# Choosing experts inside the attention stage ahead of the mixture of experts

## The reference, cut to what matters

```python
def diffusion(x):                        # third layer, per batch of 512 tokens
    x = x + token_diffusion(ln(x)) * gamma1     # 16 heads, softmax over 512 x 512 squared distances
    x = x + channel_diffusion(ln(x)) * gamma2   # 8 heads over 32 x 32 channels
    return x

def experts(x):                          # fourth layer, all 4096 tokens
    gates = softmax(x @ gate_w)                 # 8 experts
    topw, topi = top_k(gates, 2); topw = topw / sum(topw)
    h = gelu(ln(x @ w1[e] + b1[e]))             # 256 -> 512, for the two chosen experts
    y = h @ w2[e] + b2[e]                       # 512 -> 256
    return ln(sum_k(topw_k * y_k) + x)
x = x + ln(diffusion(ln(x)))
x = x + ln(experts(ln(x)))
```

## Time and profile before

| | |
|---|---|
| time, median of 3 runs | 4168.49 us (4158.25 to 4170.33) |
| the profiled execution | 4168.6 us, its span 4166.9 us |
| mean granted TensorE clock | 0.945 |
| attention stage, one body of the loop | 96.00 us |
| attention stage, last body, then drain | 90.80 us, 75.20 us |
| choosing and plan, until the first block's rows are there | 116.00 us |
| the 71 blocks | 301.20 us |
| the end | 108.90 us |

### The profile page before, as it was taken

The page is one execution under the profiler, slowest core; times in us unless marked ns, Lnnn a source line. Parts: engine busy times, 40 slices in busy tenths (PEclk is TensorE's granted clock), DMA queues, the critical chain, the costliest instruction groups (busy, mean ns, idle before and its releaser), DMA issues. The chain is left out here.

```text
span 4166.9 us, 60620 instructions
## 1 busy us (share of the span) xinstructions
PE 3688.9 (89%) x17520; PEld 2216.1 (53%) x17520; DVE 2369.6 (57%) x6484; ACT 1793.6 (43%) x4090; POOL 1671.9 (40%) x1891
## 2 busy tenths in 40 slices
PE   6999999999869999899899989858999999649994
PEld 3556655565535555555455555534555555346664
DVE  6677777677556564233656633426666666355555
ACT  2445454455435555111455541114555555304444
POOL 2343434333366675001666632421222221265664
PEclk8999999999889999999999999978999999859997
DMA  6655765566211111354011121122222221049983
GB/s 103 73 75 65 96 85 80 66 87 83 48 53 36 40 50 61 132 197 170 26 41 50 42 71 61 56 64 74 58 68 62 57 62 43 29 148 305 316 277 121
DMA packets 224948, 378.27 MB, mean 91 GB/s; under 512 B 39212, under 2 KB 156401, under 8 KB 218321
## 3 DMA queue, kind: packets, MB, share of 16 engines
q1 hardware_dynamic: 208832, 352.04, 35.7%
q0 software_dynamic: 6480, 17.77, 1.1%
q10 hardware_dynamic: 9408, 5.78, 0.5%
HBM read 170.16 MB, written 85.26 MB: 61 GB/s over the span
## 5 line engine op out<-in xcount | busy, mean ns | idle before, releaser
L758 DVE CUSTOM_DVE_ANT_0 a_ps<-a_ps,a_mask 128x128 f32<-128x128 f32 (+3 forms) x1024 | 479.6, 512 | 197.1 <-PE a_ps L513 179.4
L368 POOL TENSOR_SCALAR_AFFINE_SELECT a_probs_c<-a_probs_c 128x256 f32<-128x256 f32 (+1 forms) x384 | 188.2, 506 | 668.8 <-ACT a_probs_c L663 668.2
L2479 ACT ACTIVATE c_probsT<-c_ps 128x512 f32<-128x512 f32 x512 | 298.8, 601 | 332.9 <-PE c_ps L2301 323.6
L2618 DVE TENSOR_REDUCE c_neg_max<-c_ps 128x1 f32<-128x512 f32 x512 | 337.0, 683 | 156.0 <-PE c_ps L2289 154.5
L663 ACT ACTIVATE a_probs_c<-a_ps 128x512 f32<-128x512 f32 x640 | 345.2, 602 | 101.6 <-PE a_ps L531 71.5
L513 PE MATMUL a_ps<-a_packed_qk 65*128 65x128 f32 (+3 forms) x1024 | 339.3, 375 | 46.2 <-DVE a_maxima L758 26.0
L1094 POOL TENSOR_TENSOR w_probs<-w_probs,w_inv 128x1024 f32<-128x1024 f32 x128 | 242.5, 1895 | 334.2 <-DVE w_inv L1457 334.2
L549 PE MATMUL a_ps<-a_probs_c,a_v 128*64 128x512 f32 (+3 forms) x2048 | 317.9, 454 | 1.1 <-POOL a_probs_c L368 0.8
L531 PE MATMUL a_ps<-a_packed_qk 67*128 67x512 f32 (+3 forms) x1024 | 289.1, 345 | 2.6 <-DMA a_packed_qk<-a_max_half 2.6
L1349 ACT ACTIVATE w_probs<-w_ps_s,w_neg_max 128x256 f32<-128x256 f32 x512 | 236.3, 479 | 67.3 <-DVE w_neg_max L1452 66.6
L2289 PE MATMUL c_ps<-c_packed_qk 68*128 68x512 f32 x512 | 254.4, 501 | 11.5 <-DVE c_neg_max L2618 7.2
(11 more groups left out here) (347 smaller groups left out, 8062.6 us busy)
## 6 DMA issues: line engine op xcount, KB each, us to landing
a_packed_qk<-a_halves SPq DMA_DIRECT2D x512, 128.0 KB, 4.6
d_w<-in_L_ffn_second SPq DMA_DIRECT2D x71, 516.0 KB, 4.9
d_w<-in_L_ffn_first SPq DMA_DIRECT2D x71, 512.0 KB
rows_dram<-f_zeros SPq DMA_DIRECT2D x8, 4128.0 KB
c_packed_qk<-c_halves SPq DMA_DIRECT2D x256, 128.0 KB, 2.4
w_v<-w_v_next SPq DMA_DIRECT2D x16, 1024.0 KB, 4.6
d_rows<-rows_dram SPq DMA_DIRECT2D x71, 129.0 KB
y_dram<-w_out SPq DMA_DIRECT2D x16, 512.0 KB, 3.3
```

The costliest lines, as they stand in the source:

```text
L758: last = nc.vector.tensor_tensor_reduce(tile, tile, mask[:, (NT - 1 - i) * P:], 1.0, -3e38, ALU.add, ALU.max, accum_out=maxima_of[:, hd // ...
L2479: nc.scalar.activation(probsT[:, q % 2, r, :], ps_again[u % 2][:, :], ACT.Exp).then_inc(exp_done.sem, 1)
L2618: nc.vector.tensor_reduce(neg_max[:, g % 2, 0, s % GS:s % GS + 1], bank("s", s)[:, :], AX.X, ALU.max, negate=True).then_inc(max_ready.sem, 1)
```

## The change

For batches 0 to 6 the choosing is taken out of the mixture stage and hung on the steps of the attention stage, two batches behind: in the body of batch b the experts of batch b-2 are chosen. So bodies 2 to 7 choose for batches 0 to 5, and the drain, which has the same steps, for batch 6. Batch 7 is chosen at the start of the mixture stage, by the same functions. New kinds in the tables: T statistics, N norm (DVE), H transposes of the normed tokens (PE, copied by ACT) and G gate passes (PE), S selection (DVE), P exponential of the weights (ACT), R ranks (PE), L places (DVE). H, G and R write to the ring of 4 banks. POOL has `root_input` behind `make_h` and the 8 scatters between `root_between` and `norm_output`; SP loads the stored batch's tokens (`load_tokens`) between `store` and `load_residual`. The loop of `batches` is written out in every engine's stream. The nine loads of gate weights and constants move from behind the last body to ahead of body 0.

All this uses one buffer for tokens and one for normed tokens. So x[b] and h[b] of batches 0 to 6 are no longer in SBUF at the end: beside the blocks SP loads x[b] again (512 KB, at block steps 4, 12, ... 52) and DVE norms it again (4 instructions, at block steps 8b+8 to 8b+11).

```diff
-    EXTRA = {..., 16: [("m", 0, 0)], 26: [("v", 1, 0), ("t", 3, -1)], ...
+    EXTRA = {..., 16: [("m", 0, 0)], 17: [("H", 0, -2)], 19: [("H", 1, -2)], 21: [("G", 0, -2)],
+             23: [("G", 1, -2)], 26: [("v", 1, 0), ("t", 3, -1)], ..., 35: [("R", 0, -2)], ...
...
-            body(0, (0, 1))
-            with eng.Fori(1, B - 1) as b:
-                body(b, (-1, 0, 1))
-            body(B - 1, (-1, 0))
+            for b in range(B):
+                body(b, tuple(d for d in (-2, -1, 0, 1) if 0 <= b + d < B))
             drain(B)
...
                 if -1 in live:
                     store(b - 1)
+                    following.load_tokens(sp, b - 1)
                 load_residual(b)
...
+            following.ahead_sync(sp)
             body(0, (0, 1), True)
-            with sp.Fori(1, B - 2) as b:
+            for b in range(1, B - 2):
                 body(b, (-1, 0, 1), True)
             body(B - 2, (-1, 0, 1), False)
             body(B - 1, (-1, 0), False)
-            following.ahead_sync(sp)
             store(B - 1)
+            following.load_tokens(sp, B - 1)
...
                     keep(b, -1 in live)
+                if -2 in live:
+                    following.root_input(pool, b - 2)
                 if 1 in live:
...
                     root_between(ref(b, -1))
+                if -2 in live:
+                    following.scatter(pool, b - 2)
+                if -1 in live:
                     norm_output(ref(b, -1))
...
             def drain(b):
-                make_h(b - 1)
-                root_between(b - 1)
-                following.ahead_gpsimd(pool)
-                norm_output(b - 1)
+                body(b, (-2, -1))
...
-            batches(pe, before, body, lambda b: body(b, (-1,)))
+            batches(pe, before, body, lambda b: body(b, (-2, -1)))
...
             def drain(b):
-                for s in range(STEPS):
-                    step(b, s, (-1,))
-                    if s == GS * G // 2 + GS // 4:
-                        following.ahead_vector(dve)
+                body(b, (-2, -1))
...
+    def weigh_gates(pe, c, half, out):
+        if half == 0:
+            if c == 0:
+                pe.wait_ge(gates_in.sem, 16 * len(gates))
+            pe.wait_ge(hT_ready.sem, hT_ready.at(c, KD))
+        for i in range(2):
+            t = 2 * half + i
+            for k in range(KD):
+                last = nc.tensor.matmul(out[:, i * E:(i + 1) * E], hT[:, k, t * P:(t + 1) * P], gate_w[:, k, :],
+                                        start=k == 0, stop=k == KD - 1)
+        last.then_inc(gates_psum.sem, 1)
...
+            def load_again(b):
+                if b:
+                    sp.wait_ge(x_again.sem, x_again.at(b, 0))
+                sp.dma_start(x[b][:, :, :], x_v[b]).then_inc(x_again.sem, 16)
...
+                if s % 8 == 4 and s // 8 < B - 1:
+                    load_again(s // 8)
...
+                if 8 <= s < 8 * B and s % 8 < NT:
+                    norm_again(s // 8 - 1, s % 8)
```

More of the change, by code:

```diff
@@ L2572, in body @@
                     step(b, s, live)
-            batches(act, before, body, lambda b: body(b, (-1,)))
+            batches(act, before, body, lambda b: body(b, (-2, -1)))
         @block.vector
@@ L2727, in extras @@
                         channel_weights(at)
+                    elif kind == "T":
+                        following.input_stats(dve, at, n)
+                    elif kind == "N":
+                        following.norm_tokens(dve, at, n)
+                    elif kind == "S":
+                        following.select(dve, at, n, [bank("G", half) for half in range(2)])
+                    elif kind == "L":
+                        following.find_places(dve, at, n, bank("R", 0))
                     elif kind == "q":
@@ new lines, in input_stats, with root_input @@
+    def input_stats(dve, c, t):
+        if t == 0:
+            dve.wait_ge(x_loaded.sem, x_loaded.at(c, 16))
+        last = nc.vector.bn_stats(stats_in[:, t, :], x_new[:, t, :])
+        if t == NT - 1:
+            last.then_inc(x_linked.sem, 1)
+            dve.wait_ge(x_linked.sem, x_linked.at(c, 1))
+            for t in range(NT):
+                last = nc.vector.bn_aggr(mv_in[:, c, t, :], stats_in[:, t, :])
+            last.then_inc(roots_in.given.sem, 1)
+    def root_input(pool, c):
+        roots_in.step(pool, c, 0, rstd_in[:, c, :], mv_in[:, c, :, 1], EPS, neg_half[:, :])
@@ new lines, in norm_tokens @@
+    def norm_tokens(dve, c, half):
+        if half == 0:
+            if c == 0:
+                dve.wait_ge(gates_in.sem, 16 * len(gates))
+                dve.wait_ge(made_pool.sem, 1)
+            else:
+                dve.wait_ge(sorted_in.sem, sorted_in.at(c, 0))
+            roots_in.wait(dve, c, 0)
+            nc.vector.tensor_copy(h_new[:, :, 0], goals[:, tiles(c)])
+        for t in (2 * half, 2 * half + 1):
+            last = normalise(nc, h_new[:, t, 1:D + 1], x_new[:, t, :], mv_in[:, c, :, :], rstd_in[:, c, :], t)
+        if half:
+            last.then_inc(h_ready.sem, 1)
@@ new lines, in turn_tokens, with copy_tokens @@
+    def turn_tokens(pe, c, k, out):
+        if k == 0:
+            pe.wait_ge(h_ready.sem, h_ready.at(c, 1))
+        for t in range(NT):
+            last = nc.tensor.transpose(out[:, t * P:(t + 1) * P], h_new[:, t, 1 + k * P:1 + (k + 1) * P], ident[:, :])
+        last.then_inc(hT_psum.sem, 1)
+    def copy_tokens(act, c, k, turned):
+        if c and k == 0:
+            act.wait_ge(gates_psum.sem, gates_psum.at(c, 0))
+        act.wait_ge(hT_psum.sem, hT_psum.at(c, k + 1))
+        nc.scalar.copy(hT[:, k, :], turned[:, :]).then_inc(hT_ready.sem, 1)
@@ new lines, in weigh_pair, with rank @@
+    def weigh_pair(act, c):
+        act.wait_ge(pair_ready.sem, pair_ready.at(c, 1))
+        nc.scalar.activation(pair[:, c, 1, :], pair[:, c, 1, :], ACT.Exp).then_inc(exp_ready.sem, 1)
+    def rank(pe, c, out):
+        pe.wait_ge(counted.sem, counted.at(c, NT))
+        nc.tensor.matmul(out[:, 0:NT * E], before_me[:, :], chosen[:, :, :].rearrange("p t e -> p (t e)"),
+                         start=True, stop=False)
+        nc.tensor.matmul(out[:, 0:NT * E], ones[:, :], counts[:, tiles(c), :].rearrange("p t e -> p (t e)"),
+                         start=False, stop=True).then_inc(rank_psum.sem, 1)
@@ L3005, in send @@
                     y[:, j % HOLD, :], None).then_inc(y_stored[j % HOLD].sem, 16)
[L3007 to L3012 removed]
+            root_input(pool, B - 1)
+            scatter(pool, B - 1)
             for j in range(2):
@@ L3310, in _ @@
+            for half in range(2):
+                norm_tokens(dve, B - 1, half)
+            for part in range(4):
+                select(dve, B - 1, part, ps_y)
+            for part in range(2):
+                find_places(dve, B - 1, part, ps_h[0])
             step = [0]
```

306 lines of the change are left out of this document (128 added, 178 removed), and 27 rows, old and new, of tables (AFTER_EXP, AFTER_MAX, BEFORE_MAX, EXTRA).

## The result

The changed kernel takes 4219.07 us (median of 5 runs, 4201.19 to 4226.82) against 4168.49 us: ratio 1.0118, 95% interval 1.0094 to 1.0142. It is slower, where I had forecast 4149 us and faster. The profiled execution is one of its longer ones: 4226.8 us, span 4225.1, mean clock 0.935 (the shortest run, of 4201.19 us, had 0.939).

A forecast was written before the change was run, and what follows sets the result against it. PE was taken to bound the attention bodies and blocks, chains the choosing and drain. 4168.6 - 75 (choosing) + 34.5 (bodies) + 12.5 (drain) + 8 (blocks) gave 4149 us; forecast's own range 4138 to 4162, 8 in 10 within 4122 to 4175.

The forecast's parts named there:

- PE bounds a body, and pays what it is given: Attention bodies: PE busy 92.19 of 96.00 us, so added PE work is paid in full, 3.55 us a body.
- its three terms for waits: Bodies: PE waits 1.0 us for late norms, 0.9 for places, 0.3 for ACT's copies and exponential, per body.
- The price of the gate passes: Bodies: 16 gate passes take PE 1.8 us, half their low-clock time, with gaps 2.0.
- Norm behind the root, 1.0 us at the doubling copy: Bodies: norms wait for POOL's root behind `make_h`; DVE 1.6 us late at the doubling copy, PE 1.0.
- Places at a dense spot, 0.9 us: Bodies: places (1.2 us) stand where DVE is dense; 0.9 us of them reaches PE.
- Scatters cost nothing in a body, "if the scatters doubled, still nothing": Bodies: eight scatters and a root, 10.2 us, fit POOL's 73 us idle, so they cost nothing.
- Sum of a body: Bodies 2 to 7: 3.55 + 1.0 + 0.9 + 0.3 = 5.75 us each, times six +34.5.
- The slower rival: Bodies: through the bank ring, DVE's 7.5 and ACT's 1.4 us stand on PE's path; 75 us, whole 4189; chance 0.10.
- Drain: Drain: batch 6's tokens load first and delay the chain of norms, transposes and sums; +12.5 us (5 to 16).
- Choosing: Mixture stage's start: 116 us become one batch's 38.1 us chain plus 3 for stalls; -75 us (-72 to -79).
- Blocks: Blocks: seven 512 KB loads cost 1.2 of each 1.6 us, norms nothing; +8 us (2 to 12).
- The rival with blocks bound by DMA: Blocks: loads delay rows and weights with interest, twice their 11 us; whole 4163 us; chance 0.07.

The follow-up runs named there:

- the version moved again: Changed kernel with 128-column gate passes, loads cut in four, POOL's root first, scatters late in bodies, norm, transposes, gate passes and ranks moved: 4140.43 us, ratio 0.9918.
- Wide passes: Changed kernel with each gate pass moving 128 columns (120 of zeros) instead of 8, and loads beside the blocks cut in four: 4169.13 us, ratio 0.9993.

## Why the prediction was wrong, step by step

*PE bounds a body, and pays what it is given.* Right as far as the runs show: in the version moved again, with the clock near that of before (0.98 and 0.99), PE is busy 26.5 us more than before, by the same passes that the sum has at 21. But I priced all of PE's work, old and new, at durations of a clock of 1.00, because the earlier trace rows has 1.00 in the steady body. That is the step that failed. There was no term for the clock, and it cost 49 us in the profile, of the 65 by which the bodies missed the forecast. The other 16 are idle time of PE, 29.7 us against the 13 that the sum has in its three terms for waits. Half of the rows to suspect it were there: PE idle less than 4 us in 96 where the clock held, and 0.83 and 0.50 where it waited more.

*The price of the gate passes.* As time, right: about 1.0 us for each eight at the upper clock, 2 us a body. Their real price was what they did to the clock, 8 columns at a time. Wide passes of the same price gave 25 to 35 us back.

*Norm behind the root, 1.0 us at the doubling copy.* Right in place and size (up to 1.00 us, in four of six bodies). The instants on the way were loose: 3203 and a root of 1.3 us make 3204.3, not 3204.8, and two copies of POOL that stand between are in no term; in the body shown the root is there 2.4 us behind the end of `make_h`.

*Places at a dense spot, 0.9 us.* Too small: PE waited 1.72 us for the maxima there (at 3178.88) in the body shown, and all its waits ahead of L2303 for maxima are 11.5 us over eight cases, up to 2.2.

*Scatters cost nothing in a body, "if the scatters doubled, still nothing".* Wrong. I looked at POOL's idle time and at POOL's waits for DVE; it is DVE that is held, 2.2 us a body, and PE behind it for 2.75. I had weighed the Trainium skill, "SBUF — State Buffer", section "SBUF: two separate sides", only for the direction in which POOL waits. The page also says that the shared pair of ports is held by one engine and blocks the other. The trace agrees that one engine is held while the other works, but not with how: the scatters are 0.30 us apart, the reciprocal waits for the last of them and 1.6 us more, and it reads PSUM.

*Sum of a body.* 5.75 forecast; in the measurement 16.6, which is 3.5 of work (the forecast's), 5 of idle time and 8 of clock. The slower rival had the bodies at 75 us and the whole at 4189; it named the wrong mechanism, for DVE's work did not come to stand on the path as a whole (its bodies' idle time is 29.7 us more for PE, not 54), but its threshold of 9.1 us a body was right, and the bodies passed it.

*Drain.* +12.5 forecast, +11.5 measured.

*Choosing.* -75 forecast with 3 us for stalls, -79.2 measured: hardly any stalls; without them the chain's 38.1 us give -78. The 3 us came from no row.

*Blocks.* +8 forecast, +20.4 measured. I had the traffic right and the delay wrong: 512 KB at once ahead of a block's rows cost waits of 1.0 to 3.3 us each, not 1.2, and short falls of the clock behind four of them. The rival with blocks bound by DMA (22 us) described this, at a chance of 0.07. Cut in four, the loads cost 5.8 us, under my 8.

*Written-out loop and gate loads.* 0, as forecast, by ratio and by idle time.

What stays open: why only the reciprocal is held by the scatters; how much of the clock's 49 us belongs to the waits and how much to the narrow passes, since one profile differs from the next by 24 us there, and each remedy alone gives back most of the loss (the medians give wide passes 25 to 35 us where the pieces stood late, and 12 where they were moved); and what the last 5.8 us of the blocks are made of.

## What to carry to other kernels

When work is moved beside an engine that bounds a stretch at its upper clock, the moved work has a second price: what it does to that clock. Read the granted clock of the stretch and of its neighbours, and ask of each new piece whether it makes the engine wait or feeds it passes with few columns; here passes could be widened with zeros at no cost in time. Cut transfers that are put ahead of a tight stream into pieces, and when POOL is given DMAs to issue, look at DVE's waits too, not only at POOL's idle time.
